# Cross attention from plain queries and keys: half-row score matmuls of two heads, one unit per query tile

## The chip, the cores and the metric

One core of a Trainium2 chip runs the kernel. The metric is the device time of one execution in microseconds; several executions are timed and the median stands. The engines are named as in the profile: PE is TensorE (matmuls, with PEld its weight loads), DVE is VectorE, ACT is ScalarE, POOL is GpSimd, SP is SyncE.

## The reference

A decoder of two layers: self attention, cross attention and feed-forward, each added to `x` (4 batches, 256 tokens, 128 wide). The change lies in the first layer's cross attention: the tokens of `x` (the latents) ask, the 512 rows of a context together with the latents answer, in 16 heads of 64.

```python
x = layer_norm(x, ln_m_g, ln_m_b)              # the context, (4, 512, 128)
lat = layer_norm(latents, ln_l_g, ln_l_b)      # (4, 256, 128)
q = lat @ Wq                                   # (4, 256, 16*64)
kv = concatenate([x, lat], axis=1) @ Wkv       # 768 keys a batch
k, v = split(kv, 2, axis=-1)                   # 16 heads of 64 each
dots = einsum('bhid,bhjd->bhij', q, k) * 64 ** -0.5
out = einsum('bhij,bhjd->bhid', softmax(dots), v)
return out.reshape(b, m, 16 * 64) @ Wout
```

## The kernel before

Each engine has its own program, written out in order by hand; semaphores tie them together, and nothing is reordered by a scheduler. What an engine waits for therefore also holds up all that stands behind it on that engine.

The cross attention goes over 8 pairs of heads (`it`, a loop on the engines whose first round is written out), and in a pair over 4 batches (`b`); a pair of heads of one batch has two units (`u`, even and odd; 64 units in all, `n = 8 it + u`). **A unit is one head** of a batch with its 256 queries. The key projection never happens: ahead of the loop `cross_operands` multiplies each head's query weights by its key weights (L543, 16 products of 64 rows, heads alternating between the two row halves) into `A_all`, and a unit's query is `lat @ A` (`queries`, L840), 128 wide, which meets the normed context `kvT` itself. Scores are needed at more than the single-pass precision, so query and context are each split into a high part in the rounded format `float32r` and a low rest, and a block of scores is three single-pass matmuls (L855 high by high, L856 high by low, L857 low by high), 384 keys each, in two column blocks `c`: six for a `half`, that is a tile of 128 queries, into its own two PSUM banks (0, 1 or 2, 3).

A unit's way: TensorE's `scores` of a half; VectorE's negated maximum over its 768 keys (L1818); ScalarE's exponential with sums (L1405); TensorE's twelve transposes of the probabilities in three chunks (`transposed`, L875, banks 4 and 5), emptied by ScalarE (chunks 0 and 2, L1396) and VectorE (chunk 1, L1844) into `xpT`. Once for a pair of units TensorE forms `weighted` (L887, 6 key tiles by 2 heads in the two column halves of the array, bank 6), turns round the softmax's divisors (`factors`, L894), and VectorE multiplies (`results`, L1827). The values of the next batch are projected a half at a time (`values`, L847) into bank 7, and VectorE copies them out (L1823). On TensorE a unit's transposes are those of the unit before, so that its own exponentials have time. ScalarE's `queries` writes the high part of a query (L1391), VectorE's `query_low` the rest (L1807). GpSimd lays the current `A` into `acur` (L2265). After the loop `project` (L956) multiplies by `Wout`.

In the loop TensorE's order for an odd unit is: scores of half 0, the next unit's query, values, two chunks of transposes, scores of half 1, `weighted`, the last chunk, `factors`. For an even unit the query stands after the two chunks and nothing is weighted. VectorE's order has the first maximum, the copies, then the second maximum.

## Time and profile before

| | |
|---|---|
| Median of 3 runs | 941.11 us (940.72 to 942.71) |
| The profiled execution | 941.59 us, its span 939.7 us |
| TensorE busy | 847.7 us (90%), 6498 matmuls |
| VectorE busy | 561.1 us (60%) |
| ScalarE busy | 480.4 us (51%) |
| GpSimd busy | 256.1 us (27%) |
| Chain that ended last | PE 76%, ACT 7%, DVE 6% |
| Scores, L855 to L857 | 3 x 256 matmuls, 101.5 + 86.8 + 86.7 us |
| Maxima, L1818 | 128, 122.4 us |
| Exponentials, L1405 | 128, 115.5 us |

The rows are read like this. A timeline row has the start in us from the span's start, the length, the engine, the line, the operation, what it writes and reads, and how many neighbours were merged into it; in brackets the idle time just before and who ended it.
### The profile page before, as it was taken

The numbers are of one execution on the slowest core, as the hardware profiler recorded it, in microseconds if no ns is written. First come the engines' busy times: TensorE is split into PE (matmuls) and PEld (weight loads), VectorE is DVE, ScalarE is ACT, GpSimd is POOL, SyncE is SP. The second block draws the span as 40 slices with busy tenths as digits, with TensorE's granted clock in tenths as the row PEclk, the third lists the DMA queues.
The fourth block names the chain that finished last, engine by engine and source line by source line (L and its number), as shares of the span: only waits on it lengthen the run. The fifth ranks groups of instructions, "written<-read, shape, count | busy, mean of one in ns | idle before, by whom it ended". The sixth has DMA issues, their size and how long they took to land.

```text
span 939.7 us, 19518 instructions
## 1 busy us (share of the span) xinstructions
PE 847.7 (90%) x6498; PEld 695.7 (74%) x6498; DVE 561.1 (60%) x1561; ACT 480.4 (51%) x1154; POOL 256.1 (27%) x541
## 2 busy tenths in 40 slices
PE   5999879999999999999999968885897888887788
PEld 3888668888888888888888756663796566665565
DVE  3876466555655566655655347774544577666474
ACT  2455465555555555555555315664464476677141
POOL 3864120000000000000000047551075577776110
PEclk9999999999999999999999989999899899999995
DMA  7000000000000000000000030001222000000000
GB/s 270 2 2 1 1 1 1 1 1 1 0 0 0 0 0 0 0 0 0 0 0 0 1 115 1 2 1 28 88 47 59 1 1 0 0 0 0 24 1 22
DMA packets 9410, 15.85 MB, mean 17 GB/s; under 512 B 816, under 2 KB 5040, under 8 KB 8976
## 3 DMA queue, kind: packets, MB, share of 16 engines
q1 hardware_dynamic: 8400, 13.23, 4.2%
q0 software_dynamic: 960, 1.97, 0.9%
q8 instruction: 30, 0.49, 0.2%
q14 instruction: 20, 0.16, 0.1%
HBM read 13.16 MB, written 2.03 MB: 16 GB/s over the span
## 4 chain that ended last, share of the span: by engine, by line
PE 76%; ACT 7%; DVE 6%; issue 6%; POOL 3%; DMA 1%; ACTq 1%; DVEq 0%; POOLq 0%; SPq 0%
PE psum L875 9%; PE psum L887 9%; PE psum L855 5%; PE psum L856 5%; PE psum L857 5%; PE psum L847 5%; PE psum L598 4%; ACT arena L1301 4%; PE psum L840 3%; PE psum L617 3%; PE psum L635 3%; PE psum L956 2%; PE psum L566 1%; PE psum L1034 1%; PE psum L648 1%
## 5 line engine op out<-in xcount | busy, mean ns | idle before, releaser
L1818 DVE TENSOR_REDUCE xnegmax<-psum 128x1 f32<-128x768 f32 x128 | 122.4, 956 | 139.5 <-PE psum L857 139.3
L1405 ACT ACTIVATE arena<-psum,xnegmax 128x768 f32<-128x768 f32 x128 | 115.5, 903 | 139.5 <-DVE xnegmax L1818 97.8
L2265 POOL COPY acur<-A_all 128x128 f32 (+1 forms) x18 | 5.2, 293 | 388.1 <-PE psum L840 388.1
L875 PE MATMUL psum<-pack_a,arena 128*128 128x128 f32 x768 | 106.8, 275 | 0.2 <-ACT arena L1396 0.2
L1249 ACT ACTIVATE arena<-psum 128x384 f32<-128x384 f32 (+1 forms) x128 | 69.5, 546 | 71.2 <-PE psum L620 42.1
L855 PE MATMUL psum<-kv_high,xq_high 128*128 128x384 f32 x256 | 101.5, 396 | 1.8 <-DVE kv_low L1813 1.6
L875 PEld LDWEIGHTS psum<-pack_a,arena 128*128 128x128 f32 x768 | 87.5, 141 | 13.9 <-issue 12.3
L1396 ACT ACTIVATE arena<-psum 128x512 f32<-128x512 f32 x128 | 75.9, 593 | 42.5 <-PE psum L875 42.5
L887 PE MATMUL psum<-arena,xv 128*64 128x256 f32 x768 | 89.9, 383 | 0.0
L856 PE MATMUL psum<-kv_low,xq_high 128*128 128x384 f32 x256 | 86.8, 339 | 0.0
L857 PE MATMUL psum<-kv_high,xq_low 128*128 128x384 f32 x256 | 86.7, 339 | 0.0
L2179 POOL TENSOR_SCALAR kz<-slots,pack_a 128x256 fp32r<-128x256 f32 x128 | 69.4, 557 | 47.8 <-ACT slots L1240 47.8
L1301 ACT ACTIVATE arena<-arena 128x256 f32<-128x256 f32 x128 | 63.6, 498 | 35.8 <-POOL arena L2228 34.1
L887 PEld LDWEIGHTS psum<-arena,xv 128*64 128x64 f32 x768 | 52.3, 137 | 31.0 <-issue 6.0
L598 PE MATMUL psum<-kz,slots 128*128 128x256 f32 (+1 forms) x256 | 62.8, 317 | 0.8 <-POOL kz L2179 0.4
L617 PE MATMUL psum<-qs,kz 128*128 128x256 f32 (+1 forms) x256 | 60.7, 311 | 0.2 <-DVE qs L1620 0.2
L743 PE MATMUL psum<-arena 128*128 (+2 forms) x256 | 59.3, 342 | 0.0
L847 PEld LDWEIGHTS psum<-pack_v,kvT 128*128 128x128 f32 x396 | 54.6, 193 | 2.7 <-DVE xv L1823 0.9
L847 PE MATMUL psum<-pack_v,kvT 128*128 (+1 forms) x396 | 55.5, 277 | 0.7 <-DVE xv L1823 0.7
L855 PEld LDWEIGHTS psum<-kv_high,xq_high 128*128 128x128 f32 x256 | 48.5, 189 | 5.6 <-issue 1.8
L763 PE MATMUL psum<-pack_a,arena 128*128 128x128 f32 x256 | 39.1, 277 | 14.7 <-ACT arena L1311 13.5
L598 PEld LDWEIGHTS psum<-kz,slots 128*128 128x128 f32 x256 | 43.7, 193 | 10.1 <-issue 8.9
(309 smaller groups left out, 1853.6 us busy)
## 6 DMA issues: line engine op xcount, KB each, us to landing
w1all<-in_w SPq DMA_DIRECT2D x1, 2048.0 KB, 8.2
arena<-in_w SPq DMA_DIRECT2D x1, 2048.0 KB, 10.8
pack_v<-in_pack_v SPq DMA_DIRECT2D x1, 1088.0 KB, 9.0
pack_l<-in_pack_l SPq DMA_DIRECT2D x1, 1079.5 KB, 12.0
pack_q<-in_pack_q SPq DMA_DIRECT2D x1, 1024.0 KB, 6.9
pack_a<-in_pack_a SPq DMA_DIRECT2D x1, 653.0 KB, 6.1
pack_f<-in_pack_f SPq DMA_DIRECT2D x1, 556.0 KB, 9.9
x<-in_x SPq DMA_DIRECT2D x2, 256.0 KB, 3.0
```

What stands on the lines that cost most here:

```text
L598: last = mm(out[:, u * T:u * T + keys], held[:, u * P:(u + 1) * P], keys_of[:, 0:keys], start=True, stop=not a.causal)
L617: last = mm(out[:, at:at + T - later], keys_of[:, k * P:(k + 1) * P], queries[:, later:T], start=True, stop=not a.causal)
L847: last = mm(bank[7][:, k * P:(k + 1) * P], kvT[:, b, kt * P:(kt + 1) * P], wv[:, bass.ds(it * P, P)], start=True, stop=True)
L855: mm(out, xq_high[:, u % 2, tile], kv_high[:, u // 2, keys], start=True, stop=False)
L856: mm(out, xq_high[:, u % 2, tile], kv_low[:, u // 2, keys], start=False, stop=False)
L857: last = mm(out, xq_low[:, u % 2, tile], kv_high[:, u // 2, keys], start=False, stop=True)
L875: last = transpose(bank[4 + (3 * u + c) % 2][:, (2 * i + h) * P:(2 * i + h + 1) * P], xprob[:, u % 2, h * KEYS + kt * P:h * KEYS + (kt + 1 ...
L887: mm(bank[6][XD * a:XD * (a + 1), 0:T], xv[:, b, kt * P + XD * a:kt * P + XD * (a + 1)], xpT[:, b % 2, a, kt * T:(kt + 1) * T], start=(kt ...
L1301: last = activation(prob[:, j, u, :], limited[:, j, u, :], ACT.Exp, bias=negmax[:, j, u:u + 1], scale=-1.0, accum_out=sums[:, it, u * HG + ...
L1396: activation(xpT[:, (mu // 2) % 2, mu % 2, 2 * c * T:2 * (c + 1) * T], bank[4 + (3 * mu + c) % 2][:, :], ACT.Copy).then_inc(sx["pT_act"], 1)
L1405: activation(xprob[:, u % 2, half * KEYS:(half + 1) * KEYS].rearrange("p (c w) -> p c w", c=2), src, ACT.Exp, bias=xnegmax[:, u % 2, half: ...
L1818: v.tensor_reduce(xnegmax[:, u % 2, half:half + 1], banks_pair(half), AX.XY, ALU.max, negate=True)\
```

## The change

`A_all` and its 16 products go. The queries and the keys of a pair of heads are projected plainly: `queries` multiplies by 128 columns of `wq` (two heads at once, one matmul for a pair of units), and a new `keys` multiplies the split context by the split columns of `wk` in three single-pass matmuls for 384 keys, one half of a batch's keys in each unit, into bank 7, where the values have just been. ScalarE writes their high part (`cross_keys`), VectorE the low part (`keys_low`), for the next pair of units. The key weights are split once ahead (ScalarE copies, VectorE subtracts 1152 columns), and GpSimd lays the current columns into `wq_now` and `wk_now`.

**A unit is now a query tile** of 128 queries of both heads of a pair. Its `scores` are twelve matmuls of 64 rows, the two heads alternating between the row halves, each head into its own two banks; they stand in one block, which waits for both exponentials of the unit before and for `k_ready`. `weighted` is cut in two: key tiles 0 and 1 in the even unit, 2 to 5 in the odd one. `keys` waits for `v_ready` of the values of the same unit. VectorE's order has both maxima first, then the copy of transposes, the values, the query's low part, the divisors and the keys' low part.

```diff
-    def queries(it, u):
-
-        pe.wait_ge(sx["acur_ready"], it * 2 + u % 2 + 1)
-        mm(bank[6][:, T:2 * T], acur[:, u % 2, :], kvT[:, u // 2, S2:KEYS], start=True, stop=True)\
-            .then_inc(sx["q_psum"], 1)
+    def queries(it, b):
+
+        pe.wait_ge(sx["wq_ready"], it + 1)
+        mm(bank[6][:, T:2 * T], wq_now[:, :], kvT[:, b, S2:KEYS], start=True, stop=True).then_inc(sx["q_psum"], 1)
+
+    def keys(it, b, c):
+
+        pe.wait_ge(sx["wk_ready"], it + 1)
+        out, some = bank[7][:, 0:W], slice(c * W, (c + 1) * W)
+        mm(out, wk_now[:, 0, :], kv_high[:, b, some], start=True, stop=False)
+        mm(out, wk_now[:, 0, :], kv_low[:, b, some], start=False, stop=False)
+        mm(out, wk_now[:, 1, :], kv_high[:, b, some], start=False, stop=True).then_inc(sx["k_psum"], 1)
...
-    def scores(u, half):
-
+    def scores(u):
+
+        tile, slot = slice(u % 2 * P, (u % 2 + 1) * P), u // 2 % 2
         for c in range(2):
-            out, tile, keys = bank[2 * half + c][:, 0:W], slice(half * P, (half + 1) * P), slice(c * W, (c + 1) * W)
-            mm(out, xq_high[:, u % 2, tile], kv_high[:, u // 2, keys], start=True, stop=False)
-            mm(out, xq_high[:, u % 2, tile], kv_low[:, u // 2, keys], start=False, stop=False)
-            last = mm(out, xq_low[:, u % 2, tile], kv_high[:, u // 2, keys], start=False, stop=True)
-        last.then_inc(sx["score_psum"], 1)
+            some = slice(c * W, (c + 1) * W)
+            for i, (q, k) in enumerate(((xq_high, k_high), (xq_high, k_low), (xq_low, k_high))):
+                for a in range(2):
+                    head = slice(XD * a, XD * (a + 1))
+                    last = mm(bank[2 * a + c][:, 0:W], q[head, slot, tile], k[head, slot, some],
+                              start=(i == 0), stop=(i == 2))
+                    if c == 1 and i == 2:
+                        last.then_inc(sx["score_psum"], 1)
...
-    def weighted(p, b):
-        pe.wait_ge(sx["pT_dve"], p * 2 + 2)
-        pe.wait_ge(sx["pT_act"], p * 4 + 4)
-        pe.wait_ge(sx["y_done"], p + 1)
-        for kt in range(KT):
+    def weighted(p, b, tiles_of):
+        if tiles_of[0] == 0:
+            pe.wait_ge(sx["pT_act"], p * 4 + 3)
+            pe.wait_ge(sx["y_done"], p + 1)
+        else:
+            pe.wait_ge(sx["pT_dve"], p * 2 + 2)
+            pe.wait_ge(sx["pT_act"], p * 4 + 4)
+        for kt in tiles_of:
             for a in range(2):
...
             n, b, odd = it * 8 + u, u // 2, u % 2
-            weigh = odd and (prev or u > 1)
+            p = it * 4 + b
+            weigh = prev or u > 1
             behind = (prev and u == 0) or (cur and u)
+            after = it + (b + 1) // 4, (b + 1) % 4
             if cur:
-                pe.wait_ge(sx["q_ready"], n + 1)
+                if not odd:
+                    pe.wait_ge(sx["q_ready"], p + 1)
+                pe.wait_ge(sx["k_ready"], n + 2)
                 if prev or u:
-                    pe.wait_ge(sx["exp_done"], n * 2 - 1)
-                if not prev and not odd:
-                    pe.wait_ge(sx["kv_split"], b + 1)
-                scores(u, 0)
-                if odd:
-                    queries(it + (u + 1) // 8, (u + 1) % 8)
-                pe.wait_ge(sx["v_ready"], n + 2)
-                values(it + (b + 1) // 4, (b + 1) % 4, odd)
+                    pe.wait_ge(sx["exp_done"], n * 2)
+                scores(u)
             if behind:
                 transposed(n - 1, (u - 1) % 8, (0, 1), first=(not prev and u == 1))
             if cur:
+                values(*after, odd)
                 if not odd:
                     if prev or u >= 4:
-                        pe.wait_ge(sx["rb_ready"], it * 4 + b - 1)
-                        pe.wait_ge(sx["y_done"], it * 4 + b)
-                    queries(it, u + 1)
-                if prev or u:
-                    pe.wait_ge(sx["exp_done"], n * 2)
-                scores(u, 1)
-            if weigh:
-                if cur:
-                    pe.wait_ge(sx["q_ready"], n + 2)
-                weighted(it * 4 + b - 1, (b - 1) % 4)
+                        pe.wait_ge(sx["rb_ready"], p - 1)
+                        pe.wait_ge(sx["y_done"], p)
+                    queries(*after)
             if behind:
                 transposed(n - 1, (u - 1) % 8, (2,))
-            if weigh:
-                factors(it * 4 + b - 1)
+            if cur:
+                if not prev and b < 3:
+                    pe.wait_ge(sx["kv_split"], b + 2)
+                pe.wait_ge(sx["v_ready"], n + 3)
+                keys(*after, odd)
+            if weigh and not odd:
+                if cur:
+                    pe.wait_ge(sx["q_ready"], p + 2)
+                weighted(p - 1, (b - 1) % 4, range(0, 2))
+            if weigh and odd:
+                weighted(p - 1, (b - 1) % 4, range(2, KT))
+                factors(p - 1)
...
+    parts(0)
+    cross_queries(0, 0)
+    for c in range(2):
+        cross_keys(c + 1, 0, c)
+    parts(1)
+    act.wait_ge(sx["zT_dve"], 1)
+    parts(2)
+    parts(3)
+def cross_keys(count, slot, c):
+    act.wait_ge(sx["k_psum"], count)
+    activation(k_high[:, slot, c * KEYS // 2:(c + 1) * KEYS // 2], bank[7][:, 0:KEYS // 2], ACT.Copy)\
+        .then_inc(sx["k_high"], 1)
...
             n, b, odd = it * 8 + u, u // 2, u % 2
             behind = (prev and u == 0) or (cur and u)
-            if cur:
-                if odd:
-                    queries(n, u)
-                exponentials(it, n, u, 0, prev)
             if behind:
                 evacuate(n - 1, (u - 1) % 8, 0)
             if cur:
+                exponentials(it, n, u, 0, prev)
                 if not odd:
-                    queries(n, u)
+                    cross_queries(it * 4 + b + 1, (b + 1) % 2)
                 exponentials(it, n, u, 1, prev)
             if behind:
                 evacuate(n - 1, (u - 1) % 8, 2)
+            if cur:
+                cross_keys(n + 3, (b + 1) % 2, odd)
...
+    def keys_low(count, slot, c):
+        some = slice(c * KEYS // 2, (c + 1) * KEYS // 2)
+        dve.wait_ge(sx["k_high"], count)
+        v.tensor_tensor(k_low[:, slot, some], bank[7][:, 0:KEYS // 2], k_high[:, slot, some].bitcast(f32), ALU.subtract)\
+            .then_inc(sx["k_ready"], 1)
...
-            if cur:
-                maxima(n, u, 0)
-                if odd:
-                    query_low(n + 2, (u + 1) % 2)
             if not odd and (prev or u >= 4):
                 results(it * 4 + b - 2, it - (u < 4), (b - 2) % 4)
             if cur:
-                values(n + 3, (b + 1) % 4, odd)
+                maxima(n, u, 0)
+                maxima(n, u, 1)
             if (prev and u == 0) or (cur and u):
                 m, mu = n - 1, (u - 1) % 8
                 dve.wait_ge(sx["pT_psum"], m * 3 + 2)
-                v.tensor_copy(xpT[:, (mu // 2) % 2, mu % 2, 2 * T:4 * T], bank[4 + (3 * mu + 1) % 2][:, :])\
+                v.tensor_copy(xpT_of(mu, 1), bank[4 + (3 * mu + 1) % 2].rearrange("p (k a q) -> p k a q", k=2, a=2))\
                     .then_inc(sx["pT_dve"], 1)
+            if cur:
+                values(n + 3, (b + 1) % 4, odd)
+                if not odd:
+                    query_low(it * 4 + b + 1, (b + 1) % 2)
             if not odd and ((prev and u == 0) or (cur and u)):
                 dve.wait_ge(sx["exp_done"], n * 2)
                 v.tensor_copy(xrbc[:, :, :].rearrange("p h (a r) -> p (h a) r", a=2), spread(xr[:, :], XD))\
                     .then_inc(sx["rbc_ready"], 1)
             if cur:
-                if not odd:
-                    query_low(n + 2, (u + 1) % 2)
-                maxima(n, u, 1)
+                keys_low(n + 3, (b + 1) % 2, odd)
...
-    query_low(1, 0)
+    key_low(0)
+    query_low(0, 0)
     values(1, 0, 0)
     values(2, 0, 1)
-    for b in range(B):
+    for c in range(2):
+        keys_low(c + 1, 0, c)
+    for b in range(1, B):
         key_low(b)
...
```

Where a unit begins on TensorE, in the loop, an odd unit, before (`kv_high` and `kv_low` are the context's parts, `xq_high` and `xq_low` those of one head's query; ISA and REGISTER_ALU rows only set or hold a wait):

```order
L913 ISA [waits x_q_ready]
L855 MATMUL psum<-kv_high,xq_high 128x384 [waits x_exp_done]
L856 MATMUL psum<-kv_low,xq_high 128x384
L857 MATMUL psum<-kv_high,xq_low 128x384
L855 MATMUL psum<-kv_high,xq_high 128x384
L856 MATMUL psum<-kv_low,xq_high 128x384
L857 MATMUL psum<-kv_high,xq_low 128x384
L839 REGISTER_ALU
L840 MATMUL psum<-kvT,acur 128x256 [waits x_acur_ready]
```

After (`k_high` and `k_low` are the parts of two heads' keys, `xq_high` and `xq_low` those of both heads' queries):

```order
L933 ISA [waits x_k_ready]
L863 MATMUL psum<-k_high,xq_high 128x384 [waits x_exp_done]
L863 MATMUL psum<-k_high,xq_high 128x384
L863 MATMUL psum<-k_low,xq_high 128x384 x2
L863 MATMUL psum<-k_high,xq_low 128x384 x2
L863 MATMUL psum<-k_high,xq_high 128x384 x2
L863 MATMUL psum<-k_low,xq_high 128x384 x2
L863 MATMUL psum<-k_high,xq_low 128x384 x2
```

Six matmuls became twelve of half the rows, and ahead of them stands a new wait for `k_ready`; the query that followed the block is gone from the odd unit.

Further on in the same unit on TensorE, from the values on, before (`pack_v` holds the value weights, `pack_a` the identity of the transposes):

```order
L921 REGISTER_ALU
L847 MATMUL psum<-pack_v,kvT 128x128 [waits x_v_ready]
L847 MATMUL psum<-pack_v,kvT 128x128 x2
L862 REGISTER_ALU
L875 MATMUL psum<-pack_a,arena 128x128 [waits x_pT_dve,x_exp_done]
L875 MATMUL psum<-pack_a,arena 128x128 x3
L875 MATMUL psum<-pack_a,arena 128x128 [waits x_pT_act]
L875 MATMUL psum<-pack_a,arena 128x128 x3
L855 MATMUL psum<-kv_high,xq_high 128x384 [waits x_exp_done]
```

After (`wk_now` holds the current key weights, `xv` the values that `weighted` reads):

```order
L851 MATMUL psum<-pack_v,kvT 128x128 x3
L874 REGISTER_ALU [waits x_exp_done]
L883 MATMUL psum<-pack_a,arena 128x128 [waits x_pT_act]
L883 MATMUL psum<-pack_a,arena 128x128 x3
L952 REGISTER_ALU
L843 MATMUL psum<-kv_high,wk_now 128x384 [waits x_wk_ready,x_v_ready]
L844 MATMUL psum<-kv_low,wk_now 128x384
L845 MATMUL psum<-kv_high,wk_now 128x384
L894 ISA
L895 REGISTER_ALU [waits x_pT_dve]
L898 MATMUL psum<-arena,xv 64x256 [waits x_pT_act]
L898 MATMUL psum<-arena,xv 64x256 x7
```

The transposes' first chunks now come ahead of the values, no second block of scores follows them, and between the last chunk and `weighted` stand the three key matmuls with a wait for `v_ready`.

VectorE in the loop, the end of an even unit and an odd one, before (`xnegmax` is the negated maximum, `xv` the values, the arena copy is chunk 1 of the transposes):

```order
L1807 TENSOR_TENSOR xq_low<-psum,xq_high 128x256 [waits x_q_high]
L1817 REGISTER_ALU
L1818 TENSOR_REDUCE xnegmax<-psum 128x1 [waits x_score_psum]
L1817 ISA
L1818 TENSOR_REDUCE xnegmax<-psum 128x1 [waits x_score_psum]
L1807 TENSOR_TENSOR xq_low<-psum,xq_high 128x256 [waits x_q_high]
L1822 REGISTER_ALU
L1823 COPY xv<-psum 128x384 [waits x_v_psum]
L1843 ISA
L1844 COPY arena<-psum 128x512 [waits x_pT_psum]
L1817 REGISTER_ALU
L1818 TENSOR_REDUCE xnegmax<-psum 128x1 [waits x_score_psum]
```

After, one odd unit:

```order
L1850 ISA
L1851 TENSOR_REDUCE xnegmax<-psum 128x1 [waits x_score_psum]
L1850 REGISTER_ALU
L1851 TENSOR_REDUCE xnegmax<-psum 128x1 [waits x_score_psum]
L1873 ISA
L1874 COPY arena<-psum 128x2x2x128 [waits x_pT_psum]
L1855 REGISTER_ALU
L1856 COPY xv<-psum 128x384 [waits x_v_psum]
L1840 TENSOR_TENSOR k_low<-psum,k_high 128x384 [waits x_k_high]
```

The two maxima stand together at the head of the unit; the copy of transposes, then the values, then the keys' low part follow them.

## Rows read from the trace of the kernel before

**Rows 1.** Stretches: length, busy PE, PEld, DVE, ACT, POOL (count), PEclk, DMA.

```profile
132.00:528.00 396.00, 395.41 (x2850) 341.99 (x2850) 239.68 (x416) 215.29 (x478) 4.69 (x16) 1.00 0.00 0
735.00:885.00 150.00, 123.95 (x1049) 96.67 (x1047) 98.50 (x442) 92.82 (x308) 97.61 (x228) 1.00 0.01 3
```

**Rows 2.** Waits, 150 to 526 us: who waited for whom, total, times, longest.

```profile
DVE xnegmax L1818 <- PE psum L857: 137.4, 91, 3.7
```

**Rows 3.** TensorE's timeline: first score matmul of units 4 and 62.

```profile
154.21 0.42 PE L855 MATMUL psum<-kv_high,xq_high 128*128 128x384 f32 x1
...
514.32 0.42 PE L855 MATMUL psum<-kv_high,xq_high 128*128 128x384 f32 x1
```

**Rows 4.** TensorE's timeline, unit 31 into 32: start, us, engine, line, operation, count.

```profile
321.44 0.59 PE L840 MATMUL psum<-kvT,acur 128*128 128x256 f32 x2
321.87 0.83 PE L847 MATMUL psum<-pack_v,kvT 128*128 x6
322.53 1.04 PE L875 MATMUL psum<-pack_a,arena 128*128 128x128 f32 x8
323.32 0.42 PE L855 MATMUL psum<-kv_high,xq_high 128*128 128x384 f32 x1
...
324.28 0.34 PE L857 MATMUL psum<-kv_high,xq_low 128*128 128x384 f32 x1
324.55 2.81 PE L887 MATMUL psum<-arena,xv 128*64 128x256 f32 x24
...
327.29 0.66 PE L875 MATMUL psum<-pack_a,arena 128*128 128x128 f32 x4
...
327.93 0.42 PE L855 MATMUL psum<-kv_high,xq_high 128*128 128x384 f32 x1
...
328.90 0.34 PE L857 MATMUL psum<-kv_high,xq_low 128*128 128x384 f32 x1
329.08 0.83 PE L847 MATMUL psum<-pack_v,kvT 128*128 x6
```

**Rows 5.** TensorE's timeline at the start of the cross attention.

```profile
117.35 2.06 PE L543 MATMUL psum<-pack_q 64*128 64x128 f32 x32
119.33 1.09 PE L557 MATMUL psum<-pack_a,ctx_x 128*128 128x128 f32 x8
```

**Rows 6.** VectorE's timeline in unit 32.

```profile
329.28 0.96 DVE L1818 TENSOR_REDUCE xnegmax<-psum 128x1 f32<-128x768 f32 x1 [3.66 <-PE psum L857]
330.15 0.41 DVE L1827 TENSOR_TENSOR arena<-psum,xrb 128x256 f32 x1
330.48 0.55 DVE L1823 COPY xv<-psum 128x384 f32<-128x384 f32 x1
330.95 0.68 DVE L1844 COPY arena<-psum 128x512 f32<-128x512 f32 x1
331.55 0.17 DVE L1849 RECIPROCAL xr<-xsums 128x4 f32<-128x4 f32 x1
```

**Rows 7.** VectorE's timeline at the start of the cross attention.

```profile
124.91 0.92 DVE L1557 TENSOR_SCALAR z<-z,stat 128x128 f32<-128x128 f32 x4 [1.04 <-POOL stat L2158]
126.65 0.81 DVE L1798 TENSOR_SCALAR kvT<-psum,pack_b 128x512 f32<-128x512 f32 x1 [0.83 <-PE psum L519]
...
129.03 0.55 DVE L1823 COPY xv<-psum 128x384 f32<-128x384 f32 x1
...
131.08 3.56 DVE L1813 TENSOR_TENSOR kv_low<-kvT,kv_high 128x768 fp32r<-128x768 f32 x4
134.55 0.95 DVE L1818 TENSOR_REDUCE xnegmax<-psum 128x1 f32<-128x768 f32 x1
```

**Rows 8.** TensorE's timeline there.

```profile
129.63 0.94 PE L847 MATMUL psum<-pack_v,kvT 128*128 128x128 f32 x6 [0.73 <-DVE xv L1823]
```

**Rows 9.** Groups by line and form: count, busy us, mean ns, idle before.

```profile
L1405 ACT ACTIVATE arena<-psum,xnegmax 128x768 f32<-128x768 f32 x128 | 115.5, 903 | 139.5 <-DVE xnegmax L1818 97.8 <-PE psum L875 41.7
...
L1249 ACT ACTIVATE arena<-psum 128x384 f32<-128x384 f32 x64 | 31.4, 492 | 43.1 <-PE psum L620 42.1
```

More of the change, by code:

```diff
@@ L116, in decoder @@
         x = sb("x", [P, NT, D])
+        with nc.sbuf_tensor("k_high", [P, 2, KEYS], f32r) as k_high, nc.sbuf_tensor("k_low", [P, 2, KEYS], f32r) as k_low:
+            pass
         z = sb("z", [P, NT, D])
@@ L535, in cross_operands @@
             def cross_operands():
-                pe.wait_ge(loaded["q"], 16)
-                for h in range(XH):
-                    r = slice(XD * (h % 2), XD * (h % 2) + XD)
-                    c = slice((h // 2) * D, (h // 2 + 1) * D)
-                    bk, s = 2 + 2 * (h % 2) + h // 8, (h // 2) % 4
-                    last = mm(bank[bk][:, s * P:(s + 1) * P], col("q", "wqT")[r, c], col("q", "wkT")[r, c],
-                              start=True, stop=True)
-                    if s == 3:
-                        last.then_inc(prep_psum, 1)
                 pe.wait_ge(loaded["ctx"], 16)
@@ L902, in cross @@
                     values(0, 0, half)
+                pe.wait_ge(sx["kv_split"], 1)
+                for c in range(2):
+                    pe.wait_ge(sx["v_ready"], 2)
+                    pe.wait_ge(sx["k_ready"], c) if c else None
+                    keys(0, 0, c)
                 def body(it, prev, cur):
@@ L1336, in cross @@
             def cross():
-                for i in range(4):
-                    odd, late = i % 2, i // 2
-                    act.wait_ge(prep_psum, 3 + i)
-                    activation(A_all[:, 8 * late + odd:8 * late + odd + 7:2, :], tiles(bank[2 + 2 * odd + late][:, :]),
-                               ACT.Copy, scale=XD ** -0.5).then_inc(prep_act, 1)
-                activation(A_all[:, XH:XH + 2, :], psum[:, 2:5:2, 0:P], ACT.Copy, scale=XD ** -0.5)\
-                    .then_inc(prep_act, 1)
+                act.wait_ge(loaded["q"], 16)
+                activation(wk_all[:, 0, :], col("q", "wk"), ACT.Copy).then_inc(sx["wk_high"], 1)
                 for i in range(8):
                     c = i % 4
-                    act.wait_ge(prep_psum, 7 + i)
+                    act.wait_ge(prep_psum, 3 + i)
                     if i < 4:
@@ L1860, in cross_units @@
                 v.memset(xrb[:, 0:1], 0.0).then_inc(sx["y_done"], 1)
-                query_low(1, 0)
+                key_low(0)
+                query_low(0, 0)
                 values(1, 0, 0)
                 values(2, 0, 1)
-                for b in range(B):
+                for c in range(2):
+                    keys_low(c + 1, 0, c)
+                for b in range(1, B):
                     key_low(b)
```

71 lines of the change are left out of this document (37 added, 34 removed).

## The prediction, made before the changed kernel had run

> **What bounds the kernel now.** I read the stretches first, then who waited, then the timeline of one pair of units. From 132 to 528 us, the cross attention, TensorE is busy 395.4 of 396.0 us at the full 2.4 GHz while VectorE has 240 and ScalarE 215 [rows 1]. In that stretch it is VectorE that waits for TensorE's scores, 137 us in 91 waits [rows 2], never the other way round by more than a fraction. So today a microsecond off TensorE is a microsecond off the time, up to the point where VectorE's or ScalarE's answer comes too late. Unit 4 begins at 154.21 and unit 62 at 514.32 [rows 3]: 29 pairs of units, **12.42 us a pair**. The profiled execution took 941.59 us (1.9 outside the span), 0.5 above the median of 941.11 against which I predict.
>
> **What TensorE loses and gains per pair.** Six full-row score matmuls take 1.15 us from first start to the next block (327.93 to 329.08): 0.09 to enter and 0.177 each [rows 4]. Before, a pair has 24 of them. After, it has 24 of half the rows, two heads alternating in the two row halves. The trace has that form once: the 32 records of L543 (64 rows, halves alternating) go from 117.35 to 119.33, 1.98 us or 0.062 a record [rows 5], while the full-row 128-column records of L847 need 0.66/6 = 0.11 [rows 4]. So row halves run side by side, and 24 half-row matmuls cost 12 x 0.177: 2.12 us fewer. One of two query matmuls goes: 0.43 (321.44 to 321.87 [rows 4]). Added are six full-row key matmuls, 6 x 0.177 + 2 x 0.09 = 1.24, and one more entry and exit of the weighted product, now cut in two: about 0.19 (0.27 into L887 where 0.18 is usual, and as much out [rows 4]). Taken alone TensorE falls by 1.1 to **11.3 us a pair**.
>
> **What the new order makes it wait for.** This decides. Bank 7 now takes a unit's values and then its keys, so the keys wait for VectorE to have emptied the values, and VectorE does that after both maxima and a copy of transposes. Also, the next scores wait for the low part of those keys. Before, a unit's scores came in two blocks and maxima were spread; now both maxima start together when the scores end. Counted from a unit's first score matmul:
> First maximum at 1.35 (327.93 [rows 4] to 329.28 [rows 6]; six pairs as six matmuls). Next VectorE instruction after a maximum: 0.87 (329.28 to 330.15), twice. After the copy of transposes: 0.60 (330.95 to 331.55). The values copy itself: 0.55 [rows 6]. From its end to TensorE: 0.05 (129.03 + 0.55 to 129.63 [rows 7, 8]). **Keys start at 4.29.** TensorE gets there at 1.15 + 0.09 + 1.20 (twelve transposes, 0.79 for eight and half that again) + 0.67 (values) + 0.43 (query, even units only) = 3.54 in an even unit, 3.11 in an odd one [rows 4], so it **stands 0.75 and 1.18 us**. What stands behind the waiting key matmul is all of TensorE's queue: the weighted product, then the next scores.
> Even unit, then: the last key matmul starts 0.44 later and takes 0.34; a hop 0.04 (328.90, the sixth score, + 0.34 to 329.28); ScalarE's high part of 384 columns 0.49 (L1249's form of that width [rows 9]); hop 0.04; the low part on VectorE 0.55 (as the copy of 384 columns [rows 6]); hop 0.05: 4.29 + 1.95 = **6.25**. TensorE itself would be done earlier: keys 0.63, two of six steps of the weighted product 0.09 + 2.74/3 + 0.1 = 1.1 [rows 4]: 6.02. ScalarE has by then 2 exponentials (0.90 each [rows 9]), two evacuations and a query: it is just free.
> Odd unit: 4.29 + 0.63 + four steps (0.09 + 1.83 + 0.1) + factors (0.64 for four transposes and the factors, 327.29 to 327.93, less 0.44): **7.1**; here the keys' low part is covered by the longer weighted product.
> **Pair: 13.35, against 12.42: +0.93, on 30 pairs +28 us.** TensorE's saved 1.1 is turned into 1.9 of standing.
>
> **The start.** VectorE ends the latent rows at 125.83 (124.91 + 0.92), then splits the 1152 columns of the key weights: no row has that width; 768 columns take 0.89 apart (3.56/4), so 1.3, with bounds 0.89 and 1.8 [rows 7]. Its kvT step (0.81 at 126.65) moves from 127.46 to 127.95. The 16 products of L543 (1.98) vanish ahead, but the latents were not waiting for TensorE, so I give nothing for them. Queries, values and their two copies follow as before, 0.5 later, plus 0.89 for the first low part, partly under the query: values empty at 131.7 where they were at 131.16. New: two key blocks one after the other, 1.95 each, to 135.6; then VectorE does the other three low parts (0.89 each), which were ahead of the scores before: first maximum at 138.3 instead of 134.55 [rows 7], **+3.75**. The first units have little weighted product to cover anything: unit 1 starts 2.34 + 1.95 after that maximum, units 1 and 2 take 6.25, unit 3 7.1: unit 4 at 162.2 instead of 154.21 [rows 3], **+8** in all with the 3.75. GpSimd copies weights once per pair of heads, two units ahead of need: nothing. The larger load of the query and key weights lies 100 us before its use: nothing. The drain swaps 0.9 of weighted product to before the first half of the projection: nothing.
> Sum: 941.1 + 8 + 28 = **977 us**.
>
> **A rule against rows.** Going from scores (full width) to the weighted product (two column halves) costs 0.09 more than the usual 0.18, and about as much back [rows 4]. The Trainium skill, "TensorEngine Tiling (Array Packing)", Key Properties, says that a change of tiling mode drains the engine; were that the recorded 0.34 of the matmul in flight instead of 0.18, each change would cost 0.16, and the six on the path of a pair would give some 0.4 more, 990 us. The rows show 0.09, so I keep 977; the rule's time lies in the range. The same page, PSUM Bottleneck, warns that tiling speeds up TensorE but not what empties PSUM: the rows [rows 6] agree, and it speaks against this change.
>
> **Rivals.**
> (1) *The wait for bank 7 is hidden, faster.* If the keys found bank 7 empty on arrival, TensorE's 11.3 a pair would rule: 30 x -1.1 = -34, start +4: **911 us**. It decides from where VectorE's four instructions (0.87 + 0.87 + 0.60 + 0.55) take less than the 1.8 to 2.2 us that TensorE has between scores and keys; break-even needs each unit's chain 0.6 shorter. For it speaks only that VectorE is 60% busy in this stretch; against, that its order is fixed and the maxima are 0.87 each. 0.07.
> (2) *Row halves do not overlap in this form* (the rows of L543 are plain float32, the scores are the rounded kind, three times as wide). Then a score block costs 12 x 0.177, 1.06 more per unit on the chain, 64 times: 977 + 68 = **1045 us**. L543's 0.062 against 0.11 speaks against. 0.06.
> (3) *TensorE's standing lowers its clock.* From 735 to 885 us it is busy 124 of 150 us and has the full clock throughout [rows 1]; after, some 85%. Half clock over a tenth of the stretch would add about 19 us (6 of 13.35 us a pair are TensorE's): **996**, inside the range. 0.06.
>
> **How the numbers follow.** Main case 0.81: 977. Its bounds: no entry costs at all and a cheaper start, 12.9 a pair, 960; hops and switches 0.3 dearer a pair and a half-clocked start, 988; with (3) up to 1003. Range **958 to 1003**. It leaves out (1), (2) and little else. Within 0.2% (about what a measurement of this kernel can tell from no change) the time falls only where the standing happens to be 1.2 us a pair shorter than worked out: 0.02. Faster 0.08, slower 0.90.
>
> **What would show it.** Right: key matmuls whose idle time ends on the values copy, about 0.75 and 1.2 us by turns, one in each of the 64 units; even units' scores released by the keys' low part; 13.3 a pair; score pairs starting within some ns of each other, a block of six in 1.1 to 1.2; TensorE near 85% at full clock. Wrong if the keys start below 3.7 us after their unit's scores, if score blocks last 2.1, or if the granted clock falls.

## The result, and the profile after

The changed kernel takes **989.05 us** (median of 4 runs, 988.84 to 991.79), the kernel before 941.63 beside it (940.72 to 942.71): a ratio of 1.051, interval 1.0488 to 1.0532. It is slower, by 47 us where the forecast said 36, and inside the forecast's range. The profiled execution took 991.79 us with a span of 990.0; where its 2.7 us above the median lie, this one trace can't tell.

The page of the changed kernel: busy time of each engine, the granted clock in 40 slices, the chain that ended last.

```profile
PE 845.9 (85%) x6600; PEld 645.7 (65%) x6600; DVE 582.2 (59%) x1596; ACT 498.9 (50%) x1184; POOL 257.0 (26%) x541
...
PEclk9999959999999999999999997999789899999896
...
PE 59%; issue 12%; DVE 12%; ACT 11%; POOL 3%; DMA 1%; DVEq 1%; ACTq 1%; SPq 0%; POOLq 0%
```

TensorE is as busy in all as before (845.9 us against 847.7), but it now holds 59% of the chain that ended last, where it held 76%; VectorE and ScalarE have 23% instead of 13%. The sixth slice, 124 to 149 us, has half clock. The loop and the start, as stretches of the changed kernel (columns as in [rows 1]):

```profile
125.00:142.00 17.00, 11.36 (x42) 8.85 (x43) 9.86 (x18) 4.82 (x8) 0.64 (x2) 0.50 0.00 0
167.00:560.00 393.00, 350.07 (x2718) 258.71 (x2716) 232.20 (x406) 212.31 (x463) 5.55 (x16) 1.00 0.00 0
```

In the loop TensorE is busy 89% where [rows 1] have 99.9%; the clock stays full. Who waited for whom between 167 and 560 us of the changed kernel (total us, times, longest):

```profile
PE psum L843 <- DVE xv L1856: 34.7, 56, 0.8
PE psum L863 <- DVE k_low L1840: 6.9, 29, 0.3
```

These two waits did not exist before: the key matmuls for the values' copy, in 56 of the 58 units, and the scores behind each of the 29 even units for the keys' low part. VectorE's own wait for scores, 137.4 us in [rows 2], is down to 51.3. One even and one odd unit on TensorE in the changed kernel, and the first scores of units 4 and 62 (a row x2 holds two matmuls, one of each head):

```profile
166.19 0.44 PE L863 MATMUL psum<-k_high,xq_high 64*128 64x384 f32 x2
...
342.85 0.44 PE L863 MATMUL psum<-k_high,xq_high 64*128 64x384 f32 x2
...
343.83 0.34 PE L863 MATMUL psum<-k_high,xq_low 64*128 64x384 f32 x2
344.10 1.09 PE L883 MATMUL psum<-pack_a,arena 128*128 128x128 f32 x8
345.02 0.83 PE L851 MATMUL psum<-pack_v,kvT 128*128 x6
345.69 0.60 PE L837 MATMUL psum<-kvT,wq_now 128*128 128x256 f32 x2
346.13 0.60 PE L883 MATMUL psum<-pack_a,arena 128*128 128x128 f32 x4
347.14 0.45 PE L843 MATMUL psum<-kv_high,wk_now 128*128 128x384 f32 x1 [0.41 <-DVE xv L1856]
...
347.87 1.08 PE L898 MATMUL psum<-arena,xv 128*64 128x256 f32 x8
349.19 0.45 PE L863 MATMUL psum<-k_high,xq_high 64*128 64x384 f32 x2 [0.24 <-DVE k_low L1840]
...
353.48 0.44 PE L843 MATMUL psum<-kv_high,wk_now 128*128 128x384 f32 x1 [0.82 <-DVE xv L1856]
...
354.20 1.95 PE L898 MATMUL psum<-arena,xv 128*64 128x256 f32 x16
356.08 0.44 PE L905 MATMUL psum<-pack_a,xrbc 128*128 128x128 f32 x2
356.44 0.44 PE L863 MATMUL psum<-k_high,xq_high 64*128 64x384 f32 x2
...
560.39 0.45 PE L863 MATMUL psum<-k_high,xq_high 64*128 64x384 f32 x2
```

The even unit runs from 342.85 to 349.19, the odd one to 356.44: 6.35 and 7.25. The keys start 4.29 us after their unit's first score in both. Unit 4 starts 12.0 us later than in [rows 3] and unit 62 46.1 us later: 34.1 over 29 pairs, 1.18 each, so 13.60 a pair for 12.42. VectorE's side of the even unit:

```profile
344.20 1.82 DVE L1851 TENSOR_REDUCE xnegmax<-psum 128x1 f32<-128x768 f32 x2 [0.29 <-PE psum L863]
345.94 0.68 DVE L1874 COPY arena<-psum 128x512 f32<-128x512 f32 x1
346.54 0.55 DVE L1856 COPY xv<-psum 128x384 f32<-128x384 f32 x1
...
348.50 0.56 DVE L1840 TENSOR_TENSOR k_low<-psum,k_high 128x384 fp32r<-128x384 f32 x1 [0.67 <-ACT k_high L1391]
```

Two maxima, the copy of transposes, the copy of values: the last ends at 347.09 and TensorE's keys start at 347.14. The low part ends at 349.06 and the next scores start at 349.19. The start on TensorE in the changed kernel:

```profile
133.40 0.66 PE L843 MATMUL psum<-kv_high,wk_now 128*128 128x384 f32 x1 [0.70 <-issue]
133.85 0.52 PE L844 MATMUL psum<-kv_low,wk_now 128*128 128x384 f32 x1
134.17 0.52 PE L845 MATMUL psum<-kv_high,wk_now 128*128 128x384 f32 x1
...
138.47 0.69 PE L863 MATMUL psum<-k_high,xq_high 64*128 64x384 f32 x2 [1.26 <-DVE k_low L1840]
```

Key matmuls stand 0.32 apart here, 0.17 in the loop: half clock.

### The profile page after: what moved, and what is told of

Its sections match the earlier page's. It is cut to its first block, busy times and chain, and to the rows that moved or that the text cites. A ratio compares the mean times of both kernels' runs of the same rounds, so it can differ in the third digit from the quotient of the medians.

```text
span 990.0 us, 19939 instructions
## 1 busy us (share of the span) xinstructions
PE 845.9 (85%) x6600; PEld 645.7 (65%) x6600; DVE 582.2 (59%) x1596; ACT 498.9 (50%) x1184; POOL 257.0 (26%) x541
## 4 chain that ended last, share of the span: by engine, by line
PE 59%; issue 12%; DVE 12%; ACT 11%; POOL 3%; DMA 1%; DVEq 1%; ACTq 1%; SPq 0%; POOLq 0%
PE psum L863 9%; PE psum L898 6%; PE psum L883 4%; PE psum L595 3%; ACT arena L1319 3%; PE psum L614 3%; PE psum L632 3%; PE psum L851 3%; DVE arena L1874 2%; DVE k_low L1840 2%; PE psum L843 2%; ACT arena L1419 2%; PE psum L837 2%; PE psum L974 1%; DVE xv L1856 1%
## 5 line engine op out<-in xcount | busy, mean ns | idle before, releaser
L1851 DVE TENSOR_REDUCE xnegmax<-psum 128x1 f32<-128x768 f32 x128 | 116.6, 952 | 58.1 <-PE psum L863 58.1
L883 PE MATMUL psum<-pack_a,arena 128*128 128x128 f32 x768 | 109.0, 279 | 0.3 <-ACT arena L1419 0.3
L2299 POOL COPY wq_now<-pack_q 128x128 f32 (+1 forms) x9 | 2.6, 292 | 366.4 <-PE psum L837 364.2
L898 PE MATMUL psum<-arena,xv 128*64 128x256 f32 x768 | 97.0, 388 | 0.0
L1840 DVE TENSOR_TENSOR k_low<-psum,k_high 128x384 fp32r<-128x384 f32 x66 | 36.8, 558 | 70.8 <-ACT k_high L1391 70.8
L898 PEld LDWEIGHTS psum<-arena,xv 128*64 128x64 f32 x768 | 49.4, 136 | 34.3 <-issue 8.7
L843 PE MATMUL psum<-kv_high,wk_now 128*128 128x384 f32 x66 | 29.5, 447 | 41.5 <-DVE xv L1856 35.9
L863 PE MATMUL psum<-k_high,xq_high 64*128 64x384 f32 x256 | 51.1, 392 | 11.0 <-DVE k_low L1840 9.8
L760 PE MATMUL psum<-pack_a,arena 128*128 128x128 f32 x256 | 40.0, 281 | 14.7 <-ACT arena L1329 13.5
L851 PEld LDWEIGHTS psum<-pack_v,kvT 128*128 128x128 f32 x396 | 51.4, 198 | 1.6 <-DVE xv L1856 0.9
L1860 DVE TENSOR_TENSOR arena<-psum,xrb 128x256 f32 (+1 forms) x32 | 13.6, 425 | 63.3 <-ACT xrb L1412 63.3
```

The costliest lines, as they stand in the source:

```text
L851: last = mm(bank[7][:, k * P:(k + 1) * P], kvT[:, b, kt * P:(kt + 1) * P], wv[:, bass.ds(it * P, P)], start=True, stop=True)
L863: last = mm(bank[2 * a + c][:, 0:W], q[head, slot, tile], k[head, slot, some], start=(i == 0), stop=(i == 2))
L883: last = transpose(bank[4 + (3 * u + c) % 2][:, (2 * i + a) * P:(2 * i + a + 1) * P], xprob[:, u % 2, a * KEYS + kt * P:a * KEYS + (kt + 1 ...
L898: mm(bank[6][XD * a:XD * (a + 1), 0:T], xv[:, b, kt * P + XD * a:kt * P + XD * (a + 1)], xpT[:, b % 2, a, kt * T:(kt + 1) * T], start=(kt ...
L1851: v.tensor_reduce(xnegmax[:, u % 2, half:half + 1], banks_pair(half), AX.XY, ALU.max, negate=True)\
```

## The experiments

The theory: the two new waits cost the loop near 2 us a pair; row halves do run side by side; the start's 12 us are longer work there. Against it stand that a missing overlap of the halves or the switches between array forms set the time (rival 2 and the rule in the prediction), and that TensorE's own work would be short enough to win if the waits went (rival 1).

### The values' copy ahead of the transposes' copy

```diff
                             maxima(n, u, 1)
+                        if cur:
+                            values(n + 3, (b + 1) % 4, odd)
                         if (prev and u == 0) or (cur and u):
...
-                        if cur:
-                            values(n + 3, (b + 1) % 4, odd)
```

> VectorE copies the values out before its copy of transposes, in every unit; nothing else moves. If the hand-over of bank 7 sets the time: keys start 3.7 us after their unit's first score instead of 4.29; the odd unit falls from 7.25 to about 6.65, the even one from 6.35 only to about 6.25, because ScalarE is not free for the keys' high part before 5.1; 12.9 a pair, about 965 us. If half-row matmuls, changes of tiling or the number of TensorE instructions set it, or the round from scores over maxima to exponentials does: no change, 989 within 3.

Measured: 973.87 us (969.66 to 975.65), ratio 1.0318 (1.0273 to 1.0362). The keys start 3.70 after the scores, not 4.29; odd units take 6.65, even ones still 6.35. TensorE in this kernel, end of an even unit and keys of the odd one:

```profile
339.17 1.08 PE L898 MATMUL psum<-arena,xv 128*64 128x256 f32 x8 [0.32 <-DVE xq_low L1833]
340.70 0.44 PE L863 MATMUL psum<-k_high,xq_high 64*128 64x384 f32 x2 [0.46 <-DVE k_low L1840]
...
344.39 0.45 PE L843 MATMUL psum<-kv_high,wk_now 128*128 128x384 f32 x1 [0.24 <-DVE xv L1856]
```

Shown: the values' copy is what the keys wait for, and moving it 0.59 forward moves them 0.59. The odd unit keeps the gain. The even one gives it back: `weighted` now stands for the query's low part, and the next scores stand longer for the keys' low part. Shorten one of VectorE's answers and the next in its row is late.

### The odd unit's scores without a wait for the new keys

They don't use them; only the unit after does.

```diff
-                            pe.wait_ge(sx["k_ready"], n + 2)
+                            if not odd:
+                                pe.wait_ge(sx["k_ready"], n + 2)
...
                         if cur:
 
+                            if odd:
+                                pe.wait_ge(sx["k_ready"], n + 2)
                             values(*after, odd)
```

> The odd unit's wait for the keys' low part is moved from before its scores to before its values, which alone need bank 7 back. If the keys' way through ScalarE and VectorE is what ends the even unit: the even unit falls from 6.35 to about 6.05, where TensorE's own work ends, the odd one stays at 7.25; about 980 us. If something else releases the odd unit's scores (the exponentials): no change, 989 within 3.

Measured: 979.7 us (977.0 to 987.66), ratio 1.04 (1.0344 to 1.0456), even units 6.03, odd 7.25. In this kernel the scores of the odd unit start at 342.05, while VectorE is still at the low part that they used to wait for (to 342.24):

```profile
341.68 0.56 DVE L1843 TENSOR_TENSOR k_low<-psum,k_high 128x384 fp32r<-128x384 f32 x1 [0.69 <-ACT k_high L1394]
342.05 0.44 PE L863 MATMUL psum<-k_high,xq_high 64*128 64x384 f32 x2
```

The second wait is worth 0.3 a pair, and the even unit's 6.03 without it meets the prediction's 6.02 for TensorE itself. Two errors cancel there: the keys take 0.72 for 0.63, the two weighted steps 1.02 for 1.1.

### The two heads one after the other in a block

```diff
-                        for i, (q, k) in enumerate(((xq_high, k_high), (xq_high, k_low), (xq_low, k_high))):
-                            for a in range(2):
+                        for a in range(2):
+                            for i, (q, k) in enumerate(((xq_high, k_high), (xq_high, k_low), (xq_low, k_high))):
```

> The scores' twelve matmuls in another order: in each column block the three of one head, then the three of the other, so that neighbours lie in the same row half. If alternating row halves run side by side and this is the change's gain: a score block goes from 1.15 to about 2.2 us, and since it lies on the way to the first maximum the time rises by some 1.06 x 64, to about 1057 us. If half-row matmuls run one after the other anyway or the engine finds partners further ahead: the same 989.

Measured: 989.11 us (one run), and units of 6.35 and 7.25: no change. TensorE in this kernel, the first half of a block:

```profile
342.46 0.46 PE L863 MATMUL psum<-k_high,xq_high 64*128 64x384 f32 x2
342.74 0.35 PE L863 MATMUL psum<-k_low,xq_high 64*128 64x384 f32 x2
342.91 0.35 PE L863 MATMUL psum<-k_high,xq_low 64*128 64x384 f32 x2
```

The rows still hold pairs, one matmul of each head, most of them 6 to 25 ns apart (half of them 13 or more) and 0.17 from pair to pair, though in the program three of one head now stand before three of the other. So this did not take the overlap away, and another experiment had to.

### Both heads in one row half

```diff
-                                head = slice(XD * a, XD * (a + 1))
+                                head = slice(0, XD)
```

> Both heads' score matmuls take the first head's rows, so all twelve lie in one row half; the second head's scores are then the first head's again, with the same count, sizes, banks and waits. If two row halves run side by side and one alone does not: a block of scores goes from 1.15 to about 2.2 us (12 x 0.177), all of it ahead of the first maximum, and the time to about 989 + 64 x 1.06 = 1057. If half-row matmuls are quick for another reason (half the rows), the block stays near 1.15 and the time at 989.

Measured: 1056.73 us (one run), units of 7.40 and 8.12. TensorE in this kernel:

```profile
347.09 0.61 PE L863 MATMUL psum<-k_high,xq_high 64*128 64x384 f32 x2
347.55 0.51 PE L863 MATMUL psum<-k_low,xq_high 64*128 64x384 f32 x2
347.90 0.51 PE L863 MATMUL psum<-k_high,xq_low 64*128 64x384 f32 x2
```

Two matmuls now take 0.35, one 0.177 after the other. Row halves are what makes the block short, and rival 2's price (1.06 a unit) is nearly right: 1.05 in the even unit, 0.87 in the odd one. That the total, 67.7 us, meets the 68 is in part luck: the 29 pairs from unit 4 to unit 62 give 55.6, and 10.4 lie ahead of unit 4, more than the 4.2 of four units. The changed kernel pays none of it.

### The weighted product whole, in the odd unit

```diff
-                        if weigh and not odd:
+                        if weigh and odd:
                             if cur:
-
                                 pe.wait_ge(sx["q_ready"], p + 2)
-                            weighted(p - 1, (b - 1) % 4, range(0, 2))
-                        if weigh and odd:
-                            weighted(p - 1, (b - 1) % 4, range(2, KT))
+                            weighted(p - 1, (b - 1) % 4, range(KT))
```

> The weighted product of a pair whole in the odd unit, as before the change, instead of two steps in the even and four in the odd unit. If the even unit ends on the keys' way and not on TensorE, the two steps cost nothing there and 0.87 in the odd unit: even 6.35, odd about 8.1, about 1017 us. If TensorE's work alone set both units: the sum stays and the time falls by one entry and exit, some 0.2 a pair, to about 983.

Measured: 1021.28 us (one run), units of 6.34 and 8.12. The even unit is no shorter without its two steps: TensorE stood there anyway. So the cut of `weighted` earns 0.87 a pair in the changed kernel. Two stretches of this kernel, one of the dips of its clock and the loop, then the first scores of the odd unit with that dip and of the unit behind it:

```profile
200.00:205.00 5.00, 4.42 (x26) 3.99 (x27) 2.95 (x4) 1.64 (x4) 0.00 (x0) 0.66 0.00 0
...
167.00:590.00 423.00, 356.19 (x2688) 271.59 (x2686) 232.89 (x404) 212.62 (x462) 5.14 (x15) 0.96 0.00 0
...
200.58 0.44 PE L863 MATMUL psum<-k_high,xq_high 64*128 64x384 f32 x2 [1.26 <-DVE k_low L1833]
...
209.65 0.44 PE L863 MATMUL psum<-k_high,xq_high 64*128 64x384 f32 x2
```

The clock falls to half for 3.4 us at a time (at 201.3, 245.7, 290.1 and so on to 600.7), TensorE busy 356 of 423 us in this stretch; the changed kernel's loop has no such dip. From unit 4 to unit 62 this kernel takes 33.7 us more than the changed one. The cut accounts for 25 of them, 29 times 0.86, and the dips for 8.6: nine odd units hold one each and take 9.07 to 9.10 us, as from 200.58 to 209.65, where the other twenty take 8.10 to 8.14.

### TensorE's row written around the waits

Values copied between the maxima (even units) or right behind them (odd), the transposes split around values and keys, one step of `weighted` ahead of the odd unit's keys.

```diff
-                            transposed(n - 1, (u - 1) % 8, (0, 1), first=(not prev and u == 1))
+                            transposed(n - 1, (u - 1) % 8, (0,), first=start)
...
+                            transposed(n - 1, (u - 1) % 8, (1,), first=start)
+                        if behind and odd:
                             transposed(n - 1, (u - 1) % 8, (2,))
+                        if weigh and odd:
+                            weighted(p - 1, (b - 1) % 4, range(2, 3))
...
+                        if behind and not odd:
+                            transposed(n - 1, (u - 1) % 8, (2,))
...
                             maxima(n, u, 0)
+                        if cur and not odd:
+                            values(n + 3, (b + 1) % 4, odd)
+                        if cur:
                             maxima(n, u, 1)
```

> The changed kernel with another order in the loop and nothing else: TensorE puts the values behind the first chunk of transposes and one step of the odd unit's weighted product ahead of the keys; VectorE copies the values before its copy of transposes (in the even unit before the second maximum); the odd unit waits for the keys' low part before its values alone. If the two waits (bank 7, the keys' low part) are all that the change loses: a pair falls from 13.6 to about 11.7, some 0.7 under the kernel before, and the time to about 930. If half-row tiling, its switches or the clock cost more than the rows showed: 13 a pair at best, 970 or more.

Measured: 942.22 us (939.28 to 946.09, 12 runs) beside 942.12 for the kernel before, ratio 0.9976 (0.9944 to 1.0008). Units of 5.63 and 6.50: 12.1 a pair, not 11.7. The loop of this kernel:

```profile
164.00:514.00 350.00, 345.94 (x2720) 260.23 (x2720) 235.01 (x406) 212.52 (x464) 5.58 (x16) 1.00 0.00 0
```

TensorE is busy 98.8%. With the waits gone 1.5 us a pair come back, which shows, with the two single edits above, that they were the loss; what is left is TensorE's own work, more than the prediction had. It ends level with the kernel before and not far ahead, so rival 1's 911 us was out of reach.

### The same, with a start of its own

The first keys go to banks 2 and 3, ahead of the values; VectorE's later low parts move into the first units.

```diff
-                    keys(0, 0, c)
+                    keys(0, 0, c, 2 + c)
+                values(0, 0, 0)
+                values(0, 0, 1, 5)
```

> As the one before, and at the start the first keys go to banks 2 and 3 and the second half of the first values to bank 5, so that they do not wait for one another, and the low parts of later batches are made inside the first units. The start's 12 us over the kernel before should shrink by some 6: about 924. If the start is bound by something else (the latents, a half clock): 930.

Measured: 940.16 us (937.63 to 947.73), ratio 0.9975 (0.9939 to 1.001). Unit 4 starts at 159.39 where the run above had 163.53: 4.1 us, not 6, and the medians show 2. Unit 4 itself gives 1.7 back: it takes 7.13 us for 5.45, because its keys now stand for 1.51 us until VectorE has made a low part of the context there (L1851). Later pairs take 12.13 as above, so the loop's share of what was expected is missing here too.

### A busy start

The changed kernel with seven groups of four matmuls that nobody reads.

```diff
+            def warm():
+
+                for i in range(4):
+                    mm(bank[4][:, i * P:(i + 1) * P], ident, ident, start=True, stop=True)
```

> The changed kernel with seven groups of four idle matmuls (identity by identity, into bank 4, read by nobody) in the places where TensorE stands at the start of the cross attention; the loop is untouched. If the 4 us that the start took beyond the prediction are the half clock of 125 to 142 us, and the half clock follows from TensorE's standing: the clock stays full there and the time falls to about 985. If the groups only lie in the way: 989 to 993.

Measured: 987.25 us (985.67 to 996.29), ratio 1.0466 (1.0403 to 1.0529): by the time alone not apart from 989.05. The stretches show more. This kernel, in its profiled execution (996.29 us, the longest of the five):

```profile
118.00:135.30 17.30, 14.56 (x109) 12.78 (x108) 10.48 (x33) 8.39 (x15) 5.38 (x12) 1.00 0.01 2
...
142.00:150.00 8.00, 7.02 (x33) 6.05 (x33) 3.44 (x6) 3.45 (x7) 0.00 (x0) 0.58 0.00 0
```

At full clock the first score starts at 135.34 instead of 138.47. Then the half clock comes after all, from 142 on, and unit 4 is only 2.1 us earlier (164.05).

### Fewer parts on TensorE

The order and the start of the two reordered versions above, but the odd unit's `weighted` in one piece behind the keys, the values between the maxima in every unit, and the keys' high part ahead of ScalarE's last evacuation in odd units. The cut shows TensorE and ScalarE, against the version with its own start.

```diff
-                        if weigh and odd:
-                            weighted(p - 1, (b - 1) % 4, range(2, 3))
...
-                            weighted(p - 1, (b - 1) % 4, range(3, KT))
+                            weighted(p - 1, (b - 1) % 4, range(2, KT))
...
+                        if cur and odd:
+                            cross_keys(n + 3, (b + 1) % 2, odd)
                         if behind:
                             evacuate(n - 1, (u - 1) % 8, 2)
-                        if cur:
+                        if cur and not odd:
                             cross_keys(n + 3, (b + 1) % 2, odd)
```

> As the loop with the reordered start, but the odd unit's weighted product whole again behind the keys (one entry and exit less), made possible by VectorE copying the values between the maxima in the odd unit too, and by ScalarE making the keys' high part ahead of its last evacuation. If the reordered loop (5.63 + 6.50 a pair, TensorE busy 98.8%) is bound by TensorE's own work, what it can still lose is the 0.2 of one part: 11.9 a pair, about 934 us, under the kernel before by some 0.7%. If VectorE's later second maximum or ScalarE's order comes last: 12.1 or more, 940 and over.

Measured: **932.78 us** (930.01 to 934.7, 6 runs). Beside it the kernel before took 949.63 (941.47 to 951.69), ratio 0.984 (0.9796 to 0.9885); that median is 8 us above the ones in the other comparisons, and against 942 the gain is 1.0%. The trace supports the smaller figure: unit 62 starts at 502.71, 11.6 us ahead of [rows 3]. TensorE in this kernel, a whole odd unit, the head of the even one and its end, with VectorE's copy of the values:

```profile
342.00 0.44 PE L863 MATMUL psum<-k_high,xq_high 64*128 64x384 f32 x2
...
343.25 0.66 PE L883 MATMUL psum<-pack_a,arena 128*128 128x128 f32 x4
343.74 0.83 PE L851 MATMUL psum<-pack_v,kvT 128*128 x6
344.41 1.04 PE L883 MATMUL psum<-pack_a,arena 128*128 128x128 f32 x8
...
344.61 0.56 DVE L1861 COPY xv<-psum 128x384 f32<-128x384 f32 x1 [0.30 <-PE psum L851]
...
345.22 0.44 PE L843 MATMUL psum<-kv_high,wk_now 128*128 128x384 f32 x1
...
345.95 1.95 PE L898 MATMUL psum<-arena,xv 128*64 128x256 f32 x16
347.82 0.44 PE L905 MATMUL psum<-pack_a,xrbc 128*128 128x128 f32 x2
348.27 0.44 PE L863 MATMUL psum<-k_high,xq_high 64*128 64x384 f32 x2
...
352.88 1.08 PE L898 MATMUL psum<-arena,xv 128*64 128x256 f32 x8 [0.15 <-issue]
353.90 0.44 PE L863 MATMUL psum<-k_high,xq_high 64*128 64x384 f32 x2
```

In the odd unit no row of TensorE carries an idle time: the keys start 3.23 us after the scores, and the copy of values has ended 0.05 before (345.17), just in time. In the even unit 0.15 of idle time is left, ahead of `weighted`. This version beats both kernels: the change's idea pays once the values are copied early enough.

## Why the prediction was right or wrong

**The sign and its mechanism were right, and shown.** The keys' wait ends where the prediction put it (4.29 us after the scores, forecast 4.29), it alternates as forecast with TensorE's arrival, the even unit ends on the keys' low part, the clock stays full in the loop, and the block of twelve behaves as six. The wait itself is shorter than forecast: TensorE arrives at 3.68 us in the even unit, not 3.54 (346.13 and 0.40 for four transposes), and stands 0.61 and, in the odd unit, 1.02 us, where 0.75 and 1.18 were forecast. That costs nothing, since VectorE sets the end. Taking both waits away brings 1.5 us a pair back.

**The pair: 13.60, not 13.35**, 0.25 too little and over 29 pairs 7.3 us. The even unit is 6.35 for 6.25: the low part takes 0.56 and its way to TensorE 0.13 (349.06 to 349.19), where 0.05 was taken from the values' copy. The odd unit is 7.25 for 7.1: keys 0.72 instead of 0.63, the four weighted steps 1.88 instead of 2.02, and from the factors to the scores 0.36 instead of 0.20.

**The start: +12.0, not +8.** The durations were taken from rows at full clock, and from 125 to 142 us the clock was half, as it was from 145.6 to 149. (The kernel before had half clock too, from 132.0 to 135.4 only; the 1.00 of [rows 1] is rounded.) Queries and values took 1.6 us more (second copy done at 133.3, forecast 131.7), the two key blocks 1.1 more; the first maximum came at 141.11 (forecast 138.3), and of the remaining 1.2 up to unit 4, 1.0 lies in unit 1, which takes 7.24 us for 6.25 and holds the second stretch of half clock. With the busy start the first score came at 135.34, and the prediction's 135.6 for it was right for that clock. A half-clocked start stood only in the bound of 988, beside 0.3 dearer a pair: both came, and 989 lies at that bound. What lowers the clock there is not settled: the products of L543 are gone, and more matmuls put the fall off, but it then came later.

So 12 us separate forecast and result: 4 at the start, 7.3 in the pairs, and 0.7 that the rows don't place.

**TensorE alone: 11.3 was too low.** This set rival 1's 911 us and the expectations of the reordered loops. From start to next start, one pair in the kernel before (315.51 to 327.93) and in the last version (342.00 to 353.90), us:

| | before | last version | difference | forecast |
|---|---|---|---|---|
| scores | 4.79 | 2.51 | -2.28 | -2.12 |
| queries | 0.78 | 0.43 | -0.35 | -0.43 |
| keys | 0 | 1.36 | +1.36 | +1.24 |
| weighted | 2.74 | 2.89 | +0.15 | +0.19 |
| transposes | 2.65 | 2.92 | +0.27 | 0 |
| factors | 0.14 | 0.45 | +0.31 | 0 |
| values | 1.32 | 1.34 | +0.02 | 0 |
| pair | 12.42 | 11.90 | -0.52 | -1.12 |

What was added and removed was costed well. What failed is that two steps were costed at nothing because their work does not change: the factors are now followed by matmuls of half the rows, and in the last version the transposes come in more pieces, one of them followed by 0.15 of idle time ahead of `weighted`. A step's price hangs on what follows it on TensorE.

That is where the rule weighed in the prediction comes back. Going from the factors into the half rows costs 0.22 to 0.31 more than into full rows: 0.36 (356.08 to 356.44) to 0.45 (347.82 to 348.27), where the kernel before has 0.14, from this row to the scores at 327.93 [rows 4]:

```profile
327.79 0.38 PE L894 MATMUL psum<-pack_a,xrbc 128*128 128x128 f32 x2
```

Leaving the half rows costs 0.09 (343.83 to 344.10 is 0.27 for 0.18). From the weighted product into the half rows nothing is added: 24 of its records take 2.74 ahead of transposes [rows 4], 16 take 1.88 ahead of the factors, 8 take 1.02 ahead of the scores, which is 0.86 for each eight and 0.16 on top, whatever follows. The Trainium skill, "TensorEngine Tiling (Array Packing)", Key Properties, says that a change of tiling mode drains the engine. The entry from the factors agrees with that better than with the 0.09 the prediction took; the other entry and the exit do not. Why that one entry is dearer is open: the scores' waits stand at the same place in the program, and no run parts the two. The rule's 990 us lies near the result, but not for its reason: most switches lie where TensorE waits anyway, and the 0.16 at the odd unit's factors, 4.6 us in 29 pairs, is what they added to the path beyond the forecast.

**The rivals.** (1) fell: the keys did not find bank 7 empty, and where they hardly wait for it, 942 to 933 us result. (2) fell, with its price a unit nearly right. (3) fell in the changed kernel's loop, where the clock stayed full while TensorE stood some 1.6 us a pair for its keys. At the start the clock did fall, which was one of the prediction's signs of being wrong, and with the whole weighted product it fell in the loop too. That TensorE's standing is the reason is not shown.

## What to carry to other kernels

Work taken off a saturated engine only counts if the engines it then waits for answer sooner than it arrives: write both engines' ways to the next shared buffer from the same start, and take the later. Look first at the order on the answering engine: here one copy moved between two maxima, with TensorE's pieces arranged around it and a start rewritten, turned 5% slower into about 1% faster. Cost a start apart from the loop, with its own clock, and price each step again when its neighbour on TensorE changes form.

## What the runs showed of the hardware

- Matmuls on opposite row halves run side by side even when two more of the first half stand between them in the program: half of the pairs are 13 ns apart or more, against 4 when they alternate, and the block takes the same 1.25 us.
- A change of form on TensorE has no single price: into half rows 0.22 to 0.31 us more than into full rows from the factors, nothing more from the weighted product.
- In the loop with the whole weighted product the granted clock fell to half for 3.4 us again and again (the mean is 0.96 from 167 to 590 us), and each odd unit that it hit took 0.96 us longer; in the changed kernel's loop it stayed full for 393 us.
- The start of the changed kernel ran 17 us at half clock where the kernel before has a mean of 0.90 in the same stretch (125 to 142 us); with more matmuls ahead of it the fall came some 17 us later, and did not stay away.
